# A gather ring on GpSimd: one wait for each row gather in place of one for each group of four

## What is computed

```
h  = features @ W_layer.T + b_layer              # 6250 x 256
a1 = h @ w_a1.T + b_a1;  a2 = h @ w_a2.T + b_a2  # one number per node
v  = leaky_relu(a1[row] + a2[col])               # one number per edge, 106250 edges
ev = exp(v - segment_max(v, row)[row])
out = segment_sum((ev / segment_sum(ev, row)[row])[:, None] * h[col], row)
```

## Time and profile before

| | |
|---|---|
| median of 3 runs | 2761.94 us |
| span of the profiled execution, first to last instruction | 2728.5 us |
| the profiled execution's own total | not listed |
| GpSimd, all | 1135.7 us, 42% |
| TensorE, all | 2280.4 us, 84% |
| VectorE, all | 1795.1 us, 66% |
| ScalarE, all | 1281.0 us, 47% |
| mean granted clock of TensorE | 0.853 of full speed |
| row gathers L1140 | 878, from 355.2 to 1668.5 us |

### The profile page before, as it was taken

One profiled execution on the slowest core, in us unless ns is written; L12 is line 12 of the kernel. 1 busy time (PEld: TensorE's weight loads), 2 busy tenths in 40 slices (PEclk: granted clock), 3 DMA queues, 4 the chain that ended last, 5 costly groups with the idle time before them and its releaser, 6 DMA issues.

```text
span 2728.5 us, 47082 instructions
## 1 busy us (share of the span) xinstructions
PE 2280.4 (84%) x12485; PEld 1867.1 (68%) x12485; DVE 1795.1 (66%) x6067; ACT 1281.0 (47%) x3812; POOL 1135.7 (42%) x1159
## 2 busy tenths in 40 slices
PE   4789948888888888888888877542999999999998
PEld 2566635666666666666666654432999999999997
DVE  8678747777777777777777777653555555555553
ACT  7666645555555555555555555541222222222222
POOL 0000046666666666666666663355122211222211
PEclk8899958887787788877878788555999999999999
DMA  2344324444444344444444335563222222222221
GB/s 81 96 131 137 102 80 107 111 112 114 112 111 113 106 112 113 113 112 115 107 109 114 108 97 56 191 196 127 35 36 36 35 36 36 34 36 36 34 36 28
DMA packets 148308, 245.62 MB, mean 90 GB/s; under 512 B 27873, under 2 KB 107618, under 8 KB 147286
## 3 DMA queue, kind: packets, MB, share of 16 engines
q0 software_dynamic: 62352, 142.72, 23.2%
q1 hardware_dynamic: 85702, 99.93, 12.1%
HBM read 182.39 MB, written 60.15 MB: 89 GB/s over the span
## 4 chain that ended last, share of the span: by engine, by line
PE 59%; issue 14%; DVE 12%; another core or an unknown queue 5%; DVEq 3%; ACT 3%; POOL 1%; DMA 1%; SPq 0%; ACTq 0%; POOLq 0%
PE psum L1703 19%; PE psum L1189 14%; PE psum L1736 10%; PE psum L1180 3%; PE psum L515 3%; DVE arena L1288 3%; DVEq L1307 2%; PE psum L1197 2%; PE psum L494 1%; PE psum L1471 1%; DVE arena L1299 1%; ACT arena L586 1%; DVE arena L1332 1%; DVE arena L1271 1%
## 5 line engine op out<-in xcount | busy, mean ns | idle before, releaser
L1140 POOL DMA_INDIRECT arena<-table,arena x878 | 849.8, 968 | 478.5 <-issue 233.4
L1189 PE MATMUL psum<-arena 128*128 128x257 f32 x1756 | 679.0, 509 | 196.6 <-DVE arena L1288 113.0
L1189 PEld LDWEIGHTS psum<-arena 128*128 128x128 f32 x1756 | 362.8, 240 | 410.7 <-issue 310.9
L1288 DVE SCALAR_TENSOR_TENSOR arena<-arena,psum 128x257 f32 x878 | 421.5, 480 | 295.1 <-remote 154.3
L1703 PE MATMUL psum<-arena 128*128 128x128 f32 x4620 | 550.6, 275 | 0.6 <-ACT arena L1758 0.6
L1703 PEld LDWEIGHTS psum<-arena 128*128 128x128 f32 x4620 | 541.0, 192 | 6.7 <-issue 0.9
L1840 POOL DMA_INDIRECT out<-arena x105 | 163.1, 1554 | 665.4 <-ACT arena L1765 615.7
L1216 ACT ACTIVATE arena<-arena 128x128 f32<-128x128 bf16 x880 | 281.1, 391 | 129.7 <-DVE arena L1302 74.9
L1180 PEld LDWEIGHTS psum<-arena 128*128 128x128 f32 x1760 | 272.3, 229 | 29.0 <-issue 23.0
L1736 PE MATMUL psum<-arena 128*128 x1260 | 290.5, 379 | 0.8 <-ACT arena L1765 0.8
L1229 ACT ACTIVATE arena<-arena 128x128 f32<-128x128 bf16 x880 | 281.2, 391 | 7.1
(11 more groups left out here) (338 smaller groups left out, 3010.3 us busy)
## 6 DMA issues: line engine op xcount, KB each, us to landing
mix_inputs<-arena SPq DMA_DIRECT2D x147, 128.0 KB
arena<-table,arena POOLq DMA_INDIRECT x878
arena<-expert_in SPq DMA_DIRECT2D x105, 129.0 KB
arena<-in_x SPq DMA_DIRECT2D x98, 128.0 KB
arena<-mix_inputs SPq DMA_DIRECT2D x49, 256.0 KB
arena<-in_w SPq DMA_DIRECT2D x6, 1364.0 KB
out<-arena SPq DMA_DIRECT2D x50, 128.0 KB
table<-arena SPq DMA_DIRECT2D x49, 129.0 KB
```

The costliest lines, as they stand in the source:

```text
L1140: pool.indirect_dma_start(rows_in[j][:, q * TW:(q + 1) * TW], None, table_d[:, :], bass.IndirectOffsetOnAxis(ap=col_all[:, t:t + 1], axis=0))\
L1189: mm(psum[4 + q][:, 0:C + 1], weight[b][:, q * P:(q + 1) * P], rows_in[g][:, q * TW:q * TW + C + 1], start=True, stop=True).then_inc(S("pr ...
L1288: v.scalar_tensor_tensor(here, here, alpha[(j - 5) % RING][:, q:q + 1], psum[4 + q][:, 0:C + 1], ALU.mult, ALU.add).then_inc(S("acc_done"), 1)
```

## The change

GpSimd waited once for each group, before its first gather, until all four products of the group eight back were done. Now it waits before each gather q until product q of that group is done. `due` leaves a wait out where its value would be zero or less, in both kernels the first eight groups.

```diff
-                    if due((i - RING + 1) * G):
-                        pool.wait_ge(S("product_done"), (i - RING + 1) * G)
                     for q in range(REST if i == NG - 1 else G):
                         t = i * G + q
+                        if due((i - RING) * G + q + 1):
+                            pool.wait_ge(S("product_done"), (i - RING) * G + q + 1)
                         pool.indirect_dma_start(rows_in[j][:, q * TW:(q + 1) * TW], None, table_d[:, :],
```

## The result

The changed kernel is slower. Its median is 2791.71 us (4 runs, 2788.88 to 2800.31) against 2763.88 for the kernel before in the same session (4 runs, 2761.82 to 2766.72), a ratio of 1.0098 with an interval of 1.0077 to 1.0118, or 27 us. Forecast were 2747 us and a range up to 2780.

What follows compares the result with a forecast made beforehand. GpSimd's gather cycle, 11.96 us per eight gathers with TensorE's signals held, was taken to bound the kernel. Gain 1 (12.7) plus Gain 2 (2.5) took 15.2 us off 2761.94, giving 2747; own range 2741 to 2754, 8-in-10 range 2735 to 2780.

Steps and rivals of the forecast that it cites:

- GpSimd's cycle sets the stage: Gather stage: GpSimd's run of eight gathers plus rest, 11.96 us per two groups, paces everything though GpSimd shows 42% busy.
- Rival A: Gather stage: ring's lead hides the change, release has its own period; 2762 us, chance 0.33 shared with another no-visible-effect rival.
- 634 satisfied waits cost nothing: Added waits before gathers, already satisfied or nearly always: taken as 0 us, bounds 0 to 6 us.
- Gain 2: Very first wait on the full ring: GpSimd restarts earlier than 408.80, saving 2.5 us, bounds 0 and 2.8.
- Gain 1: Start of each run: GpSimd starts on the first product seen, not the fourth; 12.7 us, bounds 0 and 14.8.
- At the other end of a run: Where GpSimd stops: the blocked group's first product is also unseen, so runs keep eight gathers; no cost counted.
- Rival B: Row waits stop GpSimd inside a group, splitting runs; up to 106 us, priced at +35: 2797 us, chance 0.17.
- the price of one more rest: Each split of a GpSimd run costs at least 1.00 us, nearly 0 if the next rest shortens.

## Why the prediction was wrong

*That GpSimd's cycle sets the stage:* right in that the gathers set it, shown by 227 us for a quarter of them. I had read it from one repeated distance of 11.96 us. Rival A's pacemaker with a period of its own is refuted by the same run. Not right is that GpSimd's time within the cycle counts: gathers spaced wider on chip E left the cycle near 12 us, so the loop runs through the held signals and TensorE's products too. And one row said less than I took from it: the first of VectorE's two long waits in the earlier trace rows ended at 393.20, while gathers still ran, so signals are not held for the whole of a run.

*That 634 satisfied waits cost nothing:* right. With the value of before at every row the ratio is 1.0001 (0.9992 to 1.0011). The forecast's own range, 2741 to 2754, doesn't follow from its terms: with both gains at their upper bounds, 14.8 and 2.8, the sum is 2744.3, and with both at zero it is 2762.

*Gain 2, the first restart:* right in place and size, 2.8 us (405.98 against 408.80), but it is lost bit by bit, beginning with a stop of 1.29 us four gathers later.

*Gain 1, 0.12 us for each of 106 runs:* the term was a real distance. The trace's semaphore events show the four held signals of a release about 0.04 us apart, the fourth 0.13 after the first. It did not come as a gain of 12.7 us, because the runs that it was to be counted on did not stay: such a release of four products together comes 102 times before and 41 times after the change.

*"At the other end of a run ... GpSimd stops at the same place and the run still has eight gathers":* this is the step that failed. 29 of 181 runs have eight gathers after the change, and 82 have four. I had taken one stretch, in which the first product of the blocked group was already unseen, and let it stand for all 106 runs. In part the place was right (141 of 182 rests are before the first row of a group), but most come after four gathers, and 41 are inside a group. Between two profiles on chip B the same step costs 53 more rests and 30 us of gathers, where the prediction had a gain of 15.2 us. The start and the end of a run are two uses of the same wait, and I worked out only the first with numbers.

*Rival B, "GpSimd stops inside a group", 2797:* this is nearest to what happened, 2791.71, and I gave it 0.17. It had the sign and the size: more stops, at a third of 106 us, where 27 were measured. The third was a guess that came near. Its mechanism was right for a little over half of the new stops, 38 of 68 (28 of 53 on chip B); the others are at the borders of groups, where it had none. The row waits without an earlier start (1.0117, 1.0084 to 1.0150) show that a value for each row is enough for all of the cost; the early start alone (1.0067) and the waits by twos (1.0062), that two values in a group are enough for two thirds.

*Why a stop costs over 1 us after a short run too:* shown only as far as that it does (1.27 us after one gather, 1.66 after four, three-row runs 1.55), that it is no matter of bytes (0.9990) and that a group less of lead doesn't add to it (0.9992). In the prediction I had bounded the price of one more rest at 1.00 us and then let the next rest give most of it back, by the one run of four in the earlier trace rows. It is given back in part: on chip B 53 more rests come with 30 us more (1280.8 us of gathers with one wait a group, 1311.0 with the change), 0.57 us each.

*What stays open.* What holds TensorE's signals back while GpSimd gathers (whether the recording of the trace has a part in it wasn't tested either), and why GpSimd's rests are missing on chip D. Why the runs are mostly of four with a value for each row, and of eight with one for the group. Why a coarser wait is slower too (1.0075): VectorE's held wait at L1324 grows in both, but no run shows that it is the cause in either. Whether the change costs 1% on a chip like D wasn't tried; with a fill in both kernels it cost 0.28% there.

## What to carry to other kernels

A finer wait isn't only an earlier start: it is also a new place to stop, and here a stop after one gather took more than half as long as one after eight. Before splitting a wait, count the stops in the timeline and ask for each end of a run, start and stop, in every phase, what the finer value does there. And before a span is set against a median, compare the two: where they differ by more than a few microseconds, the profile is of another kind of execution, and its lengths can't be subtracted from those of the other kernel.

## What the runs showed that I had not expected

The same kernel takes 2499 us on one chip and 2730 to 2765 on four others, 10% apart. Most of it is the distance of the gathers: 1.491 in place of 1.25 us for 845 gathers is 204 of the 231 us between chip D and the profile of before, an estimate, as before wasn't profiled on D. On the four, no kernel with four gathers a group went below about 1.5 us a gather: gathers 1.25, 1.33 and 1.38 us apart end at 1.49 to 1.53 a gather, with rests that fill up the difference. On the other one the distance of the gathers is the pace, measured down to 1.35 us and inferred down to 1.25.

Signals of TensorE that VectorE and GpSimd wait for can lie for 3 us while GpSimd issues gathers, and for 6 us at L1324 after the change. By the trace's semaphore events the held ones of products come together, on average 1.65 us after the last gather of a run of eight in the kernel before, and 1.43 us after a run of four in the changed one. The Trainium skill ("DMA: Bandwidth & Descriptors", "Anatomy of one DMA — SWDGE (gpsimd) path") calls the semaphore write of a DMA nearly free. The signals that are late here are TensorE's, not a DMA's, so no run here confirms or refutes that sentence, and the prediction stretched it when it counted the 3.1 us against it.
